# Four value products of 32 rows side by side, with softmax sums from added key halves, in a vision transformer block

## The chip, the cores and the metric

The kernel runs on one core of a Trainium2 chip. The metric is the time of one execution on the device in microseconds (us). An execution has five engines that run their own instruction streams and meet at semaphores: PE (TensorE: matmuls, and PEld, its weight loads), DVE (VectorE), ACT (ScalarE), POOL (GpSimd) and SP, which here issues DMAs.

## What is computed

128 images of 224x224x3 are cut into 14x14 patches, embedded into 192 numbers each, and given a class token: 197 tokens (padded to 198 in the kernel). One transformer block follows:

```python
h = tokens(x) ; h = concatenate([cls_tok, h])            # 128 x 197 x 192
n = layernorm(h)
q, k, v = (n @ W.T in 6 heads of 32)
scores = q k^T * 32**-0.5 + lam * (q . anchor_h)         # the same for all keys of a query
attn = softmax(scores) ; h = h + (attn @ v) @ Wo.T
x8 = clip(round(layernorm(h) / 0.02), -128, 127)         # int8
h = h + (x8 @ weight_t) * (0.02 * 0.01) + bias
```

## The kernel before

**Stages.** The first stage (`build_tokens`, up to about 429 us) embeds the patches and writes `h` and the normalised `xn` to scratch in HBM. The second (`build_attention`) takes the images one after the other and is the subject here.

**Steps.** Each engine runs the same loop over `i`: unrolled steps at both ends and a hardware loop over groups of six steps between. In one step an engine works on several images at once, each at another stage: f = i+5 (load and transpose of `xn`), a pair p of images (projection of q and k), a = i+1 (scores and their maxima), b = i (transposed scores, exponentials), c = i-1 (value products, transposes back, normalisation), e = i-2 (output projection, second layer norm), g = i-3 (quantising), k = i-4 (feed-forward product, output). A pair of images is projected in three blocks of 128 columns, two of them in an odd step (L894, L905) and one in an even step (L913). The order of work on each engine is the order in which its `step` writes it out; between engines there are semaphore waits only.

**Order on PE in a step (L883 to L996).** Scores 0 and 1 of a (`score`, L834, matmul L841); in an odd step block 0 into bank MISC[2]; the last transposed score of c, `score_t(c, 5)` (L896, matmul L853); block 1 or, in an even step, block 2 into MISC[2] (`project_block`, matmul L809); score 2; feed-forward (L924); value products of c (`attend`, L858, matmul L869); `score_t(b, 0)`; score 3; output projection of e (L829 to L831); `score_t(b, 1)`; transposes back (`turn_back`, L874, L879); transposes of `xn_in` into MISC[2] (L790); score 4; `score_t(b, 2)`; transposes of `qx`; transposes of `att`; score 5; `score_t(b, 3)`; value projection (L818); `score_t(b, 4)`; transposes of the maxima `max_parts` (L994).

**Scores twice.** `score` gives queries by keys, of which DVE takes the maximum per query (L1084). DVE splits the maxima into two parts (`max_parts`, a copy L1156 and a subtract L1158 of 99x12 elements), PE turns them, ACT copies them to `max_rows`, and SP sends them as rows into `q_st`. `score_t` gives keys by queries, with the maximum taken off by those two extra rows of the contraction, against ones in `k_st`. ACT takes the exponential of it (L1011) into `probs`, 99 keys by 2 halves of keys by 198 queries. Matmuls on fp32r operands are one record in the trace; those on fp32 operands are two.

**Value products.** `attend` multiplies `probs` by `vals`, tiles of 64 columns a head: 32 values, a column of ones (whose product is the softmax sum), and zeros. Two heads go to the upper and the lower 64 partitions of a bank of `o_bank`, three pairs of heads, two halves of the keys: 12 fp32 matmuls. ACT copies the result to `o_t` (L1037, L1038), six transposes bring it back to queries by heads, DVE takes the reciprocal (L1142) and multiplies (L1146) to `att`.

**DVE in a step (L1095 to L1180).** Maxima 0 and 1; the low parts `qk_lo` of the projected blocks (L1092) with maximum 2; `y` (L1117); two instructions on `qx` of g (L1122, L1125); maximum 3; `h1` of e (L1135); reciprocal and `att` of c; maxima 4 and 5; `max_parts`; statistics `st2` of e (L1164); `x_lo` of f (L1171), which reads bank MISC[2]; `a_lo` (L1179).

**POOL in a step (L1197 to L1223).** For e alone: `hb` = `h1` + bias (L1204), then after `st2` nine small instructions of the layer norm, each waiting for the one before (`norm_factors`, L139 to L147), then two of 99x192 that write `qx` (L1222), which DVE takes up in the next step.

**ACT in a step (L1020 to L1074).** High parts of the blocks (`high`, L1018), `exps(c, 5)`, `o_t`, `exps` 0, 1, 2 of b, `x_hi`, `exps(b, 3)`, `a_hi`, `exps(b, 4)`, `max_rows`, `qx_t`, `vals`.

**Ahead of the first step.** POOL finishes the last tokens' layer norm and fills two rows of `k_st` with ones (L1237); PE waits for these and for four constants of DVE (L998, L999).

Of the kernel before, what the change touches and what calls it, by code (L numbers as in the profile page):

```python
# [5 lines left out]
F32 = mybir.dt.float32  # L6
# [37 lines left out]
EARLY = 8  # L44

# [556 lines left out]
def build_attention(nc, s):  # L602
# [13 lines left out]
    HP = H // 2  # L616
    SPLIT = H - 4
    TW = 64
    OR = TW + HD + 1

# [10 lines left out]
    q_st = tile("q_st", [ST + 2, NP, H, 2, TP], F32R)  # L631
    k_st = tile("k_st", [ST + 2, NP, H, 2, TP], F32R)


    vals = tile("vals", [TC, NS, 2, H, TW])
# [4 lines left out]
    o_t = tile("o_t", [OR, NS, HP, TP])  # L640
# [29 lines left out]
    ones_made = sem("ones_made")  # L670
    last_row_ln = sem("last_row_ln")
# [15 lines left out]
    ln2_step, hb_done, passed = sem("ln2_step"), sem("hb_done"), sem("passed2")  # L687
    LN2_PER = 11
# [18 lines left out]
    with nc.Block() as block:  # L707
        @block.sync
        def _(sp):
# [11 lines left out]
            def step(i):  # L721
# [41 lines left out]
                if a.within(B):  # L763

                    sp.wait_ge(mrow_done, a.count(1, 1))
# [19 lines left out]
        def _(pe):  # L785
# [60 lines left out]
            def score_t(n, h):  # L846

                if h == 0:
                    pe.wait_ge(max_landed[n.slot], n.landed(16))
# [8 lines left out]
            def attend(n):  # L858

                pe.wait_ge(exp_done, n.count(H, H))  # L860
                pe.wait_ge(v_done, n.count(1, 1))
                if n.reuses(1):
                    pe.wait_ge(norm_done, n.count(1, 0))
                for p in range(HP):
                    for kc in range(2):
                        kk = TC if kc == 0 else NTOK - TC
                        for half in range(2):
                            h = 2 * p + half
                            last = pe.matmul(o_bank[half * TW:(half + 1) * TW, p // 2, (p % 2) * TP:(p % 2 + 1) * TP],  # L869
                                             vals[0:kk, n.two, kc, h, :], probs[0:kk, n.two, h, kc, :],  # L870
                                             start=kc == 0, stop=kc == 1)
                last.then_inc(av_done, 1)

            def turn_back(n):  # L874

                pe.wait_ge(ot_done, n.count(2, 2))
                for c in range(2):
                    for p in range(HP):
                        last = pe.transpose(o_bank[0:TC, c, 2 * TW * p:2 * TW * p + OR],  # L879
                                            o_t[:, n.two, p, c * TC:(c + 1) * TC], ident[0:OR, 0:OR])  # L880
                last.then_inc(back_done, 1)

            def step(i):  # L883
# [11 lines left out]
                if has_c:  # L895
# [10 lines left out]
                elif has_p:  # L906
# [6 lines left out]
                    project_block(MISC[2], p, 2)  # L913
                if has_a:
# [363 lines left out]
```

## Time and profile before

| | us |
|---|---|
| median of 3 runs | 1858.71 |
| lowest, highest | 1855.8, 1861.74 |
| the profiled execution's own time | 1860.42 |
| its span, first to last instruction | 1858.7 |

Busy shares of the span: PE 93%, PEld 86%, DVE 76%, ACT 42%, POOL 40%. The page divides the span into 40 slices; from the tenth on, PE's busy digit is 9 in all but two slices (its granted clock is at 9 or 8 tenths there on the page), with DVE at 7 and ACT at 5. In the tables of the trace a row has the start in us, its length in us, the engine, the line of the kernel, the operation, output and inputs by name, and shape; in square brackets stands the engine's idle time before it and what ended that. Matmuls overlap in the pipeline, so a matmul's length is longer than its distance to the next; distances of starts are what counts for PE. A granted clock of 1.00 is 2.4 GHz.

### The profile page before, as it was taken

The page shows a single profiled execution, that of the slowest core. Times are in us where ns is not written, and L with a number is a line of the kernel's source. Part 1 is how long each engine was busy: PE and PEld are TensorE (multiplying, and loading weights), DVE is VectorE, ACT ScalarE, POOL GpSimd, SP SyncE. Part 2 cuts the span into 40 slices and gives each one's busy share as a digit, 9 for nine tenths or more (in the row PEclk, how much of TensorE's full clock was granted, in tenths as well). Part 3 has the DMA queues.
Part 4 walks back from the last instruction along what each step waited for, and adds up shares of the span by engine and source line. Part 5 has one row for each costly group of instructions (what it writes and reads, how often), then busy time and mean ns, then how long its engine had stood idle before and what let it go on. Part 6 is the DMA issues. An engine that isn't in the chain of part 4 may idle for free.

```text
span 1858.7 us, 51623 instructions
## 1 busy us (share of the span) xinstructions
PE 1737.3 (93%) x15344; PEld 1602.8 (86%) x15344; DVE 1409.2 (76%) x3646; ACT 781.9 (42%) x1878; POOL 738.7 (40%) x1909
## 2 busy tenths in 40 slices
PE   1999999993899999999999999999999999999996
PEld 1999999993788888888888888888888888888885
DVE  4888888883577777777777777777777777777773
ACT  2000000000455555555555555555555555555552
POOL 3343543453033434334343344343443433434344
PEclk8999999996899999999999999999999999999997
DMA  9789998966677777777767777777787777777751
GB/s 282 207 284 305 304 314 285 312 212 150 115 135 137 140 132 132 135 138 135 135 127 137 136 135 138 127 137 136 134 138 131 134 135 137 135 135 127 134 99 31
DMA packets 214780, 303.57 MB, mean 163 GB/s; under 512 B 47585, under 2 KB 203636, under 8 KB 204613
## 3 DMA queue, kind: packets, MB, share of 16 engines
q1 hardware_dynamic: 204686, 228.05, 63.4%
q10 hardware_dynamic: 6054, 38.54, 7.3%
q0 software_dynamic: 3984, 36.28, 5.1%
q8 instruction: 30, 0.49, 0.1%
q14 instruction: 26, 0.20, 0.0%
HBM read 126.49 MB, written 58.29 MB: 99 GB/s over the span
## 4 chain that ended last, share of the span: by engine, by line
PE 62%; DVE 7%; issue 3%; POOL 2%; ACT 1%; SPq 1%; DMA 1%; DVEq 0%; POOLq 0%
PE o_bank L869 14%; PE bank L809 10%; PE bank L853 8%; PE bank L841 6%; PE bank L790 5%; PE o_bank L879 3%; PE bank L818 3%; PE o_bank L790 3%; PE bank L829 2%; PE bank L830 2%; PE bank L831 2%; PE bank L924 2%; DVE neg_max L1084 2%; DVE x_lo L1171 2%; ACT probs L1011 1%
## 5 line engine op out<-in xcount | busy, mean ns | idle before, releaser
L1011 ACT ACTIVATE probs<-bank 99x396 f32<-99x396 f32 x768 | 383.5, 499 | 245.3 <-PE bank L853 245.0
L1084 DVE TENSOR_REDUCE neg_max<-bank 99x2 f32<-99x394 f32 x768 | 420.2, 560 | 87.4 <-PE bank L841 86.0
L321 PE MATMUL bank<-e_t,xt 128*128 128x192 f32 x2352 | 386.8, 328 | 40.7 <-DVE xt L407 21.6
L321 PEld LDWEIGHTS bank<-e_t,xt 128*128 128x128 f32 x2352 | 385.2, 191 | 41.9 <-DVE xt L407 22.7
L853 PE MATMUL bank<-q_st,k_st 98*99 98x198 f32 x1536 | 284.3, 266 | 9.4 <-DMA q_st<-max_rows 4.1
L869 PE MATMUL o_bank<-probs,vals 99*64 99x198 f32 (+1 forms) x3072 | 289.0, 336 | 0.5 <-issue 0.3
L841 PE MATMUL bank<-k_st,q_st 96*99 96x198 f32 x1536 | 271.0, 272 | 14.6 <-DMA k_st<-qk_lo 9.7
L1204 POOL TENSOR_TENSOR hb<-h,ffn_bias 99x384 f32<-99x384 f32 x128 | 128.5, 1004 | 356.6 <-DVE h L1135 356.6
L869 PEld LDWEIGHTS o_bank<-probs,vals 99*64 99x64 f32 (+1 forms) x3072 | 211.8, 137 | 48.5 <-issue 1.2
L853 PEld LDWEIGHTS bank<-q_st,k_st 98*99 98x99 f32 x1536 | 202.4, 166 | 56.9 <-issue 36.6
L407 DVE STREAM_TRANSPOSE xt<-x_t 128x256 f32<-128x256 f32 x588 | 214.9, 416 | 43.3 <-PE bank L321 42.8
L1005 ACT ACTIVATE x_hi<-bank 128x396 fp32r<-128x396 f32 x128 | 63.3, 495 | 397.2 <-PE bank L790 397.2
L841 PEld LDWEIGHTS bank<-k_st,q_st 96*99 96x99 f32 x1536 | 195.6, 167 | 24.4 <-DMA k_st<-qk_lo 10.0
L1005 ACT ACTIVATE o_t<-o_bank 97x396 f32<-97x396 f32 (+1 forms) x256 | 93.1, 416 | 285.2 <-PE o_bank L869 285.2
L1092 DVE TENSOR_TENSOR qk_lo<-bank,qk_hi 128x396 fp32r<-128x396 f32 x192 | 108.8, 567 | 71.6 <-ACT qk_hi L1018 71.6
L1222 POOL TENSOR_SCALAR qx<-h,ln 99x192 f32<-99x192 f32 x256 | 127.0, 504 | 41.0 <-POOL ln L147 41.0
L1122 DVE TENSOR_SCALAR qx<-qx 99x384 f32<-99x384 f32 x128 | 46.1, 360 | 124.3 <-POOL qx L1222 124.3
L146 POOL TENSOR_TENSOR ln<-ln,minus_half 99x2 f32<-99x2 f32 (+2 forms) x143 | 127.4, 891 | 25.4 <-POOL ln L145 25.3
L139 POOL TENSOR_TENSOR ln<-st 99x2 f32<-99x2 f32 x128 | 25.2, 197 | 277.4 <-DVE st L1164 277.4
L1018 ACT ACTIVATE qk_hi<-bank 128x396 fp32r<-128x396 f32 x192 | 96.3, 502 | 90.6 <-PE bank L809 88.0
L829 PE MATMUL bank<-wo_hi,a_hi 96*99 96x192 f32 x512 | 130.0, 254 | 0.0
L830 PE MATMUL bank<-wo_lo,a_hi 96*99 96x192 f32 x512 | 129.9, 254 | 0.0
(121 smaller groups left out, 3426.4 us busy)
## 6 DMA issues: line engine op xcount, KB each, us to landing
x_t<-in_x_dram ACTq DMA_DIRECT2D x26, 1344.0 KB, 19.3
x_t<-in_x_dram SPq DMA_DIRECT2D x26, 1344.0 KB, 21.9
q_st<-qk_hi SPq DMA_DIRECT2D x128, 198.0 KB, 4.0
k_st<-qk_hi SPq DMA_DIRECT2D x128, 198.0 KB, 4.5
xn_in<-xn_scratch SPq DMA_DIRECT2D x128, 148.5 KB
h_in<-h_scratch SPq DMA_DIRECT2D x128, 148.5 KB
h_scratch<-h_t POOLq DMA_DIRECT2D x13, 1344.0 KB, 18.4
xn_scratch<-xn_t POOLq DMA_DIRECT2D x13, 1344.0 KB, 9.1
```

The costliest lines, as they stand in the source:

```text
L321: last = pe.matmul(token_bank(p)[:, 0:D], xt[:, p, c // 3, c % 3, :], e_t[:, row_kind(t), col, c // 3, c % 3, :], start=c == 0, stop=c == 5)
L407: last = nc.vector.transpose(xt[:, p, :, c, :].rearrange("p m (g b) -> p g m b", b=32), pix[:, c])
L790: last = pe.transpose(bank[0:width, ic * TP + c * TC:ic * TP + (c + 1) * TC], src[:, at, c, ic * width:(ic + 1) * width], ident[0:TC, 0:TC])
L809: last = pe.matmul(wide(bank, BLOCK), weights[:, Q:K + 1, :].rearrange("p w n -> p (w n)")[:, cols], inputs, start=i == 0, stop=i == len(p ...
L829: pe.matmul(acc, hi, wo_hi[:, ic, :], start=ic == 0, stop=False)
L830: pe.matmul(acc, hi, wo_lo[:, ic, :], start=False, stop=False)
L841: last = pe.matmul(S_BANK[h % 2][0:TC, c * TP:(c + 1) * TP], q_st[0:ST, n.pair, h, n.two, c * TC:(c + 1) * TC], k_st[0:ST, n.pair, h, n.tw ...
L853: last = pe.matmul(T_BANK[0:TC, c * TP:(c + 1) * TP], k_st[:, n.pair, h, n.two, c * TC:(c + 1) * TC], q_st[:, n.pair, h, n.two, :], start= ...
L869: last = pe.matmul(o_bank[half * TW:(half + 1) * TW, p // 2, (p % 2) * TP:(p % 2 + 1) * TP], vals[0:kk, n.two, kc, h, :], probs[0:kk, n.tw ...
L1005: nc.scalar.activation(dst, src, ACT.Copy, **affine).then_inc(done, 1)
L1011: nc.scalar.activation(probs[:, n.two, h, :, :], wide(T_BANK, TC), ACT.Exp).then_inc(exp_done, 1)
L1084: nc.vector.tensor_reduce(out=neg_max[:, n.two, :, h], in_=wide(S_BANK[h % 2], TC)[:, :, 0:NTOK], axis=AX_X, op=ALU.max, negate=True).then ...
```

## The change

- `vals` shrinks to 32 columns a head, without ones and zeros. `attend` writes 32 partitions a product: heads 0, 1, 4, 2 side by side over the first 198 columns of one bank; heads 3 and 5 over the next 198 columns, beside two tiles of softmax sums.
- The sums: a new tile `key_sum` holds the sum of the two halves of keys of `probs`. POOL adds heads 0 and 1, and 2 and 3, of image b; DVE adds heads 4 and 5 of image c. Six products of `key_sum` with `pick` (a column of ones at place j of 32 columns, else zeros) put the sums of the heads into rows. In all 18 fp32 matmuls. The first eight wait for five exponentials only, the others for the sixth and for the sums.
- As the padded key would now be counted, it gets a third extra row of the contraction: a score of -1e30 (`q_st` set by POOL to it ahead of the first step; `k_st` rows made on POOL as `key_rows`, copied by ACT into place). PE waits for ACT's copy only at its first transposed score.
- `o_t` is one tile of 128 partitions copied by one ACT instruction; four transposes of 128 columns go to the second bank. The wait for `mrow_done` moves from the products to the transposes back, the wait for `norm_done` of the image before is dropped.
- In even steps `score_t(c, 5)` and its exponential come after block 2.
- The rows of `Wo` are permuted on the host to the new order of heads (`HEAD_AT`).

```diff
+HEAD_AT = (0, 1, 4, 2, 3, 5)
...
-    vals = tile("vals", [TC, NS, 2, H, TW])
+    vals = tile("vals", [TC, NS, 2, H, HD])
+    pick = tile("pick", [TC, HG, HD])
...
-    o_t = tile("o_t", [OR, NS, HP, TP])
+    key_rows = tile("key_rows", [ST + 3, TP])
+    key_sum = tile("key_sum", [TC, NS, H, TP])
+    o_t = tile("o_t", [TILE, NS, 2, TP])
...
             def attend(n):
-                pe.wait_ge(exp_done, n.count(H, H))
+                def add_values(at, col, kc):
+                    h = HEAD_AT[at]
+                    kk = TC if kc == 0 else NTOK - TC
+                    pe.matmul(o_bank[at % 4 * HD:(at % 4 + 1) * HD, 0, col:col + TP], vals[0:kk, n.two, kc, h, :],
+                              probs[0:kk, n.two, h, kc, :], start=kc == 0, stop=kc == 1)
+
+                pe.wait_ge(exp_done, n.count(H, H - 1))
                 pe.wait_ge(v_done, n.count(1, 1))
-                if n.reuses(1):
-                    pe.wait_ge(norm_done, n.count(1, 0))
-                for p in range(HP):
-                    for kc in range(2):
-                        kk = TC if kc == 0 else NTOK - TC
-                        for half in range(2):
-                            h = 2 * p + half
-                            last = pe.matmul(o_bank[half * TW:(half + 1) * TW, p // 2, (p % 2) * TP:(p % 2 + 1) * TP],
-                                             vals[0:kk, n.two, kc, h, :], probs[0:kk, n.two, h, kc, :],
-                                             start=kc == 0, stop=kc == 1)
+                for kc in range(2):
+                    for at in range(4):
+                        add_values(at, 0, kc)
+                for j in range(HG):
+                    if j == 0:
+                        pe.wait_ge(exp_done, n.count(H, H))
+                        pe.wait_ge(pool_sums, n.count(2, 2))
+                    if j < 2:
+                        for at in (4, 5):
+                            add_values(at, TP, j)
+                    else:
+                        pe.wait_ge(dve_sums, n.count(1, 1))
+                    for side in range(2):
+                        to = (2 + side) * HD
+                        last = pe.matmul(o_bank[to:to + HD, 0, TP:2 * TP], pick[:, j, :],
+                                         key_sum[:, n.two, HEAD_AT[side * HG + j], :], start=j == 0, stop=j == HG - 1)
                 last.then_inc(av_done, 1)
 
             def turn_back(n):
-                pe.wait_ge(ot_done, n.count(2, 2))
+                pe.wait_ge(ot_done, n.count(1, 1))
                 for c in range(2):
-                    for p in range(HP):
-                        last = pe.transpose(o_bank[0:TC, c, 2 * TW * p:2 * TW * p + OR],
-                                            o_t[:, n.two, p, c * TC:(c + 1) * TC], ident[0:OR, 0:OR])
+                    for t in range(2):
+                        last = pe.transpose(o_bank[0:TC, 1, (2 * c + t) * TILE:(2 * c + t + 1) * TILE],
+                                            o_t[:, n.two, t, c * TC:(c + 1) * TC], ident[:, :])
                 last.then_inc(back_done, 1)
...
-                if has_c:
+                if has_c and (odd or not has_p):
                     score_t(c, 5)
...
                     project_block(MISC[2], p, 2)
+                    if has_c:
+                        score_t(c, 5)
...
+            def add_keys(n):
+                dve.wait_ge(exp_done, n.count(H, H))
+                if n.reuses(NS):
+                    dve.wait_ge(av_done, n.count(1, 1 - NS))
+                nc.vector.tensor_tensor(key_sum[:, n.two, 4:H, :], probs[:, n.two, 4:H, 0, :], probs[:, n.two, 4:H, 1, :],
+                                        ALU.add).then_inc(dve_sums, 1)
...
                     maxima(a, 1)
+                if has_c and not (has_p and not odd):
+                    add_keys(c)
                 if has_p and odd:
                     low(p, 0, MISC[2])
                 elif has_p:
                     low(p, 2, MISC[2])
+                    if has_c:
+                        add_keys(c)
...
+                def add_keys(first):
+                    pool.wait_ge(exp_done, b.count(H, first + 2))
+                    if first == 0 and b.reuses(NS):
+                        pool.wait_ge(av_done, b.count(1, 1 - NS))
+                    heads = slice(first, first + 2)
+                    nc.gpsimd.tensor_tensor(key_sum[:, b.two, heads, :], probs[:, b.two, heads, 0, :],
+                                            probs[:, b.two, heads, 1, :], ALU.add).then_inc(pool_sums, 1)
+
+                if b.within(B):
+                    add_keys(0)
...
                                         ffn_bias[:].unsqueeze(1).broadcast_to([TC, 2, D]), ALU.add).then_inc(hb_done, 1)
+                if b.within(B):
+                    add_keys(2)
                 pool.wait_ge(st2_done, e.count(1, 1))
...
-            pool.memset(k_st[ST:ST + 2, :, :, :, :].bitcast(F32), 1.0).then_inc(ones_made, 1)
+            pool.memset(q_st[ST:ST + 3, :, :, :, :].bitcast(F32), NO_SCORE).then_inc(no_score_made, 1)
```

## Rows read from the trace of the kernel before

**Rows 1.** Windows: busy PE, PEld, DVE, ACT, POOL (instructions), PEclk, DMA share, GB/s.

```profile
700.00:1700.00 1000.00, 977.31 (x9565) 884.39 (x9561) 772.84 (x1931) 563.38 (x1363) 401.96 (x1131) 1.00 0.76 135
```

**Rows 2.** Timeline of PE over an odd and an even step.

```profile
1206.77 0.42 PE L809 MATMUL bank<-x_hi,wa_hi 128*128 128x396 f32 x1 [0.39 <-DVE x_lo L1171]
...
1215.28 0.41 PE L841 MATMUL bank<-k_st,q_st 96*99 96x198 f32 x2
...
1217.57 0.43 PE L853 MATMUL bank<-q_st,k_st 98*99 98x198 f32 x2
1217.91 0.42 PE L809 MATMUL bank<-x_hi,wa_hi 128*128 128x396 f32 x1
...
1224.98 0.54 PE L790 MATMUL o_bank<-ident,att 99*96 99x99 f32 x4
1225.30 0.40 PE L841 MATMUL bank<-k_st,q_st 96*99 96x198 f32 x2
...
1227.92 0.42 PE L809 MATMUL bank<-x_hi,wa_hi 128*128 128x396 f32 x1 [0.34 <-DVE x_lo L1171]
```

**Rows 3.** Timeline of DVE over the same steps.

```profile
1211.26 0.36 DVE L1122 TENSOR_SCALAR qx<-qx 99x384 f32<-99x384 f32 x1 [0.51 <-POOL qx L1222]
...
1216.63 0.61 DVE L1164 BATCH_NORM_STATS2 st<-h 99x6 f32<-99x192 f32 x2
1217.16 0.61 DVE L1171 TENSOR_TENSOR x_lo<-bank,x_hi 128x198 fp32r<-128x198 f32 x2
...
1222.41 0.36 DVE L1122 TENSOR_SCALAR qx<-qx 99x384 f32<-99x384 f32 x1 [1.27 <-POOL qx L1222]
...
1226.55 0.17 DVE L1158 TENSOR_TENSOR max_parts<-neg_max,max_parts 99x12 fp32r<-99x12 f32 x1
```

**Rows 4.** Timeline of POOL over the even step.

```profile
1217.32 0.20 POOL L139 TENSOR_TENSOR ln<-st 99x2 f32<-99x2 f32 x1 [2.31 <-DVE st L1164]
...
1221.38 0.99 POOL L1222 TENSOR_SCALAR qx<-h,ln 99x192 f32<-99x192 f32 x2 [0.31 <-POOL ln L147]
1224.19 1.01 POOL L1204 TENSOR_TENSOR hb<-h,ffn_bias 99x384 f32<-99x384 f32 x1 [1.81 <-DVE h L1135]
```

**Rows 5.** Timeline of PE, two narrow windows at the first value products.

```profile
1209.47 0.39 PE L869 MATMUL o_bank<-probs,vals 99*64 99x198 f32 x2
...
1209.47 0.56 PE L869 MATMUL o_bank<-probs,vals 99*64 99x198 f32 x4
```

**Rows 6.** The chain that ended last: start, length, what.

```profile
1207.92 0.19 PE bank L853 x2
...
1209.54 2.17 PE o_bank L869 x24
...
1213.51 0.52 PE o_bank L879 x6
```

**Rows 7.** Timeline of ACT over the two steps.

```profile
1208.35 0.49 ACT L1011 ACTIVATE probs<-bank 99x396 f32<-99x396 f32 x1
...
1223.57 0.50 ACT L1011 ACTIVATE probs<-bank 99x396 f32<-99x396 f32 x1 [0.67 <-PE bank L853]
...
1225.93 0.50 ACT L1011 ACTIVATE probs<-bank 99x396 f32<-99x396 f32 x1 [0.23 <-PE bank L853]
```

**Rows 8.** First stage: two timelines at 83 us, two lines' durations (min/median/max ns).

```profile
83.24 0.68 POOL L586 TENSOR_SCALAR xn_t<-h_t,ln 128x192 f32<-128x192 f32 x1
...
83.58 0.55 DVE L390 SCALAR_TENSOR_TENSOR wb<-w_raw,wb 64x192 fp32r<-64x192 f32 x1
...
L586 POOL TENSOR_SCALAR xn_t<-h_t,ln x3: 512/600/682, 82.8 to 83.9; 128x192 f32<-128x192 f32 x3
...
L393 DVE TENSOR_TENSOR wb<-w_raw,wb x2: 355/356/356, 77.5 to 89.9; 64x192 fp32r<-64x192 f32 x2
```

**Rows 9.** Timelines of PE and of SP at the second stage's start.

```profile
441.31 0.89 PE L790 MATMUL bank<-ident,xn_in 99*128 99x99 f32 x4 [13.91 <-POOL k_st L1237]
...
438.27 0.39 SPq L719 DMA_DIRECT2D xn_in<-xn_scratch  x1
```

More of the change, by code:

```diff
@@ L630, in build_attention @@
     qk_lo = tile("qk_lo", [BLOCK, 3, 2 * TP], F32R)
-    q_st = tile("q_st", [ST + 2, NP, H, 2, TP], F32R)
-    k_st = tile("k_st", [ST + 2, NP, H, 2, TP], F32R)
-    vals = tile("vals", [TC, NS, 2, H, TW])
+    q_st = tile("q_st", [ST + 3, NP, H, 2, TP], F32R)
+    k_st = tile("k_st", [ST + 3, NP, H, 2, TP], F32R)
+    vals = tile("vals", [TC, NS, 2, H, HD])
+    pick = tile("pick", [TC, HG, HD])
     neg_max = tile("neg_max", [TC, NS, 2, H])
@@ L763, in step @@
                 if a.within(B):
+                    if a.fixed and a.n == 0:
+                        sp.wait_ge(no_score_made, 1)
                     sp.wait_ge(mrow_done, a.count(1, 1))
@@ L1026, in step @@
                     high(p, 0, MISC[2])
-                if has_c:
+                if has_c and (odd or not has_p):
                     exps(c, 5)
@@ L1032, in step @@
                     high(p, 2, MISC[2])
+                    if has_c:
+                        exps(c, 5)
                 if has_c:
@@ L1036, in step @@
                         act.wait_ge(back_done, c.count(1, 1 - NS))
-                    copy(o_t[:, c.two, 0:2, :], o_bank[0:OR, 0, 0:2 * TP].rearrange("p (a n) -> p a n", a=2), ot_done)
-                    copy(o_t[:, c.two, 2, :], o_bank[0:OR, 1, 0:TP], ot_done)
+                    copy(o_t[:, c.two, :, :], wide(o_bank[:, 0, :], TILE), ot_done)
                 if has_b:
@@ L1072, in step @@
                         act.wait_ge(av_done, a.count(1, 1 - NS))
-                    copy(vals[:, a.two, :, :, 0:HD],
+                    copy(vals[:, a.two, :, :, :],
                          MISC[1][0:TC, 0:2 * D].rearrange("p (c h d) -> p c h d", c=2, h=H), v_done)
+            act.wait_ge(rows_made, 2)
+            copy(k_st[ST:ST + 3, :, :, :, :].rearrange("p a h s n -> p (a h s) n"),
+                 key_rows[ST:ST + 3, :].unsqueeze(1).broadcast_to([3, 2 * NP * H, TP]), ones_made)
             images(act, step)
@@ L1180, in step @@
                                             a_hi[:, c.two, :, :].bitcast(F32), ALU.subtract).then_inc(alo_done, 1)
-            nc.vector.memset(vals[:], 0.0).then_inc(consts, 1)
+            nc.vector.memset(pick[:], 0.0).then_inc(consts, 1)
             dve.wait_ge(consts, 1)
-            nc.vector.memset(vals[:, :, :, :, HD:HD + 1], 1.0).then_inc(consts, 1)
+            for j in range(HG):
+                nc.vector.memset(pick[:, j, j:j + 1], 1.0).then_inc(consts, 1)
             dve.wait_ge(last_row_ln, 9)
@@ L1223, in step @@
                                             v[6][:, cc:cc + 1], ALU.add, ALU.mult).then_inc(ln2_step, 1)
+            pool.memset(key_rows[ST:ST + 3, :], 1.0).then_inc(rows_made, 1)
+            pool.wait_ge(rows_made, 1)
+            pool.affine_select(out=key_rows[ST:ST + 3, 0:NTOK], in_=key_rows[ST:ST + 3, 0:NTOK], compare_op=ALU.is_ge,
+                               fill=0.0, base=1, pattern=[[0, NTOK]], channel_multiplier=-1).then_inc(rows_made, 1)
+            pool.wait_ge(rows_made, 2)
             made = [0]
```

30 lines of the change are left out of this document (19 added, 11 removed).

## The prediction

> **What bounds the kernel now.** I read the sums over the steady stretch first: TensorE (PE) busy 977 of 1000 us at a granted clock of 1.00, which is 2.4 GHz, the next engine at 77% [rows 1]. So PE is the first suspect; but at 98% it is full only if nothing waits, and what an edit to PE's work is worth depends on what ends each wait. So next the order of time on PE over two steps [rows 2]. Steps come in two kinds: odd ones project two blocks (L809), even ones one. I cut a pair at two marks: L809's first matmul, and the fifth score (L841, `score(a, 5)`). Odd work: 1206.77 to 1215.28 = 8.51 us; then 2.63 to the next L809 (1217.91); even work 7.39 (to 1225.30); then 2.62 (to 1227.92). A pair is 21.15 us.
>
> The two gaps of 2.62 are no PE sum. L809 starts 0.14 us after `x_lo` ends (1217.16 + 0.61 = 1217.77, [rows 3]), in both kinds of step; PE idles 0.39 and 0.34 there. `x_lo` is at the end of VectorE's queue after max, `max_parts`, `st2`. So the gap is **DVE's latency from the fifth score**.
>
> The even work of 7.39 has a second limit, a loop through three engines. From the fifth score (1215.28) `st2` is done at 1217.24; GpSimd (POOL) starts its chain 0.08 later, at 1217.32 [rows 3, 4]; chain and `qx` end at 1221.38 + 0.99 = 1222.37; DVE, idle for 1.27 us until then, starts `qx` at 1222.41; then max, h1, reciprocal and `att` lead to PE's turn of `att` at 1224.98 and the fifth score at 1225.30 [rows 2, 3]. That is 2.04 + 5.05 + 0.04 + 2.89 = 10.02 us, which is just the step (7.39 + 2.63). In even steps PE and this **loop** end together, so PE time saved there is worth nothing; in odd steps the loop has 1.1 us to spare.
>
> **The change, part by part.** *Value products.* Now 12 fp32 matmuls, recorded as 24, two side by side; a pair starts each 0.17 us (0.39, 0.56 us for 2, 4) [rows 5], 12 pair starts, 2.17 us in all [rows 6]. After it, 18 matmuls, 36 records, four side by side: two rounds of four heads, two rounds of two heads with two sums, one round of two sums. Five rounds of two records are 10 starts: 2 x 0.17 = 0.34 us less. Nothing here shows four at once; from below it is 0.34, from above 18 starts if only two run together (+1.02 us). I take the 0.34, since the two of now start together with no loss.
>
> *Transposes back.* Six took 0.52 us [rows 6]; four remain, with 128 columns for 97: between 0 and 0.17 less, I take 0.08. The single o_t copy spares ScalarE an instruction where PE has a score and the output projection before it needs the result: nothing.
>
> *The moved score.* In even steps `score_t(c, 5)` stands at 1217.57, in the time in which L809 waits for `x_lo` anyway [rows 2]. Behind L809 its 0.19 us [rows 6] is added to the even work. The wait for the exponential that it passes was not the last one ahead of L809. Cost: +0.19 even, bounds 0 and 0.19.
>
> *Key sums.* Two adds on POOL of 99x396, one on DVE. POOL takes 1.00 us for the add of 99x384 at 1224.19 [rows 4], so 1.03 each. The first waits for the second exponential of image b, which ends at 1223.57 + 0.50 = 1224.07 [rows 7]; it and `hb` behind it end by 1226.2. The second waits for the fourth, 1225.93 + 0.50 = 1226.43, so with POOL's 0.08 it starts at 1226.51 and ends at 1227.54, while the chain behind it on POOL would have started at 1227.33. That is 0.2 us on the loop. The wait has in its queue the layer norm chain, for which DVE's `qx`, and behind that all of DVE, waits. DVE's add waits for `exps(c, 5)` (1208.35 + 0.49 in odd steps, [rows 7]), with low, max and y behind it; DVE has 0.51 (odd) and 1.27 us (even) before `qx` [rows 3] and the add takes about 0.55: just covered. PE's new waits for these sums have the first score of the next image behind them; POOL's are over before the step begins, DVE's add about 0.5 us before PE's last round in even steps and 1.5 in odd ones. The wait for the maxima's row copy, moved from the products to the transposes back, is met before either place.
>
> *The collision.* POOL's second add starts at 1226.51; DVE's `max_parts` subtract (L1158), with both inputs in SBUF, starts at 1226.55 [rows 3]. What happens then is shown once in the prologue [rows 8]: a DVE instruction with two SBUF inputs, started at 83.58 among POOL's normalising of rows, took 0.55 instead of 0.36 us, and POOL's took 0.68 and 0.60 instead of 0.51. They take turns. There the DVE instruction got what was left of POOL's short one; it came free when POOL's reads were over. L1158 would stand behind nearly all of a 1.03 us add: end at 1227.55 instead of 1226.72, **0.83 us late**. Everything in DVE's queue moves with it: `st2` (so the chain), `x_lo` (so L809), `mpart_done` (so PE's transposes of maxima, which then have 0.7 us to wait).
>
> The Trainium skill, page "SBUF — State Buffer", section "Who interferes with whom", says that a DVE instruction with two SBUF inputs and a GpSimd instruction that reads SBUF exclude each other for the whole instruction, by order of issue. By it the delay is the same 0.83; with sharing by halves, which the prologue rows do not exclude for so long an add, it would be about 0.2.
>
> Who is first? POOL leads by 0.04 us, and from the two stalls in the prologue (POOL's of 0.17 in the row of 83.24, behind the DVE instruction in front of 83.58, and DVE's of 0.19 at 83.58) both engines need about equally long from a start to the first read. So I take POOL as first, in both kinds of step.
>
> *Sum.* Odd: 8.51 - 0.34 - 0.08 = 8.09 of PE work, gap 2.62 + 0.83 = 3.45: 11.54 us. Even: PE would need 7.39 + 0.19 - 0.42 + 3.45 = 10.61, the loop 10.02 + 0.83 = 10.85 (the add is over before the late chain starts): 10.85. A pair is 22.39, +1.24; 0.62 us an image. 126 of the 128 images are in this state: +78 us.
>
> *Start of the stage.* PE's wait of 13.9 us for POOL's memset of `k_st` ends at 441.31 [rows 9]. The memset leaves PE's path, but the input loads, the first image's last issued at 438.27 + 0.39, land only some 1.5 to 2 us later, and two small POOL instructions (about 0.8 us) now stand ahead of the chain that leads to them: bounds -1 and +1 us, taken as 0. The new copy on ScalarE (some 7 us) lies beside that. The memset of `q_st` is over long before the first maxima.
>
> The profiled execution was 1860.4 us, 1.7 above the median of 1858.7: 1860.4 + 78 - 1.7 = **1937 us**. If the add takes 0.99 to 1.24 us, it is 1932 to 1963.
>
> **Rivals.** (1) POOL and DVE don't disturb each other here. Then odd is 8.09 + 2.62 = 10.71; even the loop with the 0.2 of POOL, 10.22; pair 20.93, -0.22: -14 us, 1845. For it: the overlap in the prologue is only one place, and L393 ran in 0.36 us beside POOL's power. This is the **other side**, faster, and what decides is whether L1158 waits. (2) They exclude each other, but DVE is first. L1158 is on time; then DVE's new add (at about 2.1 us after L809) keeps POOL's chain waiting some 0.4 us: even loop 10.02 + 0.25 + 0.4 = 10.67, odd 10.71, pair +0.23: +14, 1873. (3) POOL first in one kind of step alone: the odd gap without the 0.83, pair +0.41: +26, 1885. (4) The POOL loop isn't a limit: odd 10.71, even 7.16 + 2.62 = 9.78: pair -0.66, -42: 1817. Against it: the 1.27 us for which DVE waits for `qx`, and `att` that PE takes 0.06 us after it could be ready. (5) Four narrow products don't run together, only two, with 18 starts. Then odd is 8.51 + 1.02 - 0.08 + 2.62 = 12.07, even 7.39 + 0.19 + 0.94 + 2.62 = 11.14, pair +2.06: +130, 1988. The gain of the products is gone from a start distance of 0.20 us on (10 x 0.20 = 12 x 0.17).
>
> On (5), the Trainium skill, page "TensorE: Matmul & The Clock Gate", section "Measured speedup vs the span model", has four row tiles at 3.07 times and three column tiles at 2.38 times one, not 4 and 3. By the first, a start of four would be 0.17 x 4 / 3.07 = 0.22 us (an estimate), over the 0.20 just named; its own model of 4 ns per further tile puts that down to fill and drain, and then nothing is lost. This trace has two only.
>
> **How the numbers follow.** Forecast 0.50 (shown interference, lead of 0.04 us). (1) 0.18. (2) 0.11. (3) 0.08. (4) 0.07. (5) 0.06. The range leaves out (4) and (5): 1843 to 1957, the top from a longer add. A measurement of this kernel tells 0.3%, 5.6 us, from no change. Faster by more: most of (1) and all of (4), 0.21. Within: rest of (1) and a part of (2), 0.07. Slower: 0.72.
>
> **What would show it.** Right: L1158 at about 1.0 us instead of 0.17, PE waiting for DVE ahead of L994, L809's idle time over 0.4 us in both kinds, steps of about 11.5 and 10.9 us; L869 with 36 records in about 1.8 us. Wrong: L1158 at 0.17 and POOL's second add longer than 1.03 (rival 2), both at their length (rival 1), L869 over 2.2 us (rival 5), DVE not waiting for `qx` in even steps (rival 4).

## The result, and the profile after

| | before | after |
|---|---|---|
| median of 4 runs, us | 1859.34 | 1912.79 |
| lowest, highest | 1855.8, 1861.74 | 1910.57, 1913.83 |
| the profiled execution's own time | 1860.42 | 1910.57 |
| its span | 1858.7 | 1909.0 |

The ratio is 1.0282 (95% interval 1.027 to 1.0294): 53.5 us slower, where 78 were forecast. The changed kernel has fewer starts of value products and is still slower, so the place to look is where PE waits. The windows row for 700 to 1700 us (busy PE, PEld, DVE, ACT, POOL with instructions; granted clock; DMA share; GB/s) answers [rows 1]:

```profile
700.00:1700.00 1000.00, 919.80 (x10122) 801.36 (x10120) 836.72 (x1952) 534.24 (x1226) 544.30 (x1274) 1.00 0.75 129
```

PE went from 977 to 920 us of 1000 at the same granted clock of 1.00, DVE from 773 to 837, POOL from 402 to 544. The timeline of PE over an even and an odd step answers [rows 2] (L817 is `project_block`, before L809; L849 `score`, before L841; L1018 the transposes of the maxima, before L994):

```profile
1200.32 0.42 PE L817 MATMUL bank<-x_hi,wa_hi 128*128 128x396 f32 x1
...
1207.28 0.55 PE L798 MATMUL o_bank<-ident,att 99*96 99x99 f32 x4
1207.60 0.41 PE L849 MATMUL bank<-k_st,q_st 96*99 96x198 f32 x2
...
1209.78 0.34 PE L1018 MATMUL o_bank<-ident,max_parts 99*12 99x99 f32 x2 [0.48 <-DVE max_parts L1197]
1210.93 0.42 PE L817 MATMUL bank<-x_hi,wa_hi 128*128 128x396 f32 x1 [0.45 <-DVE x_lo L1210]
...
1222.38 0.43 PE L817 MATMUL bank<-x_hi,wa_hi 128*128 128x396 f32 x1 [0.44 <-DVE x_lo L1210]
```

The two marks of the prediction cut it: even work 1200.32 to 1207.60 = 7.28, gap 3.33 (to 1210.93); odd work 8.12 (its fifth score, `score(a, 5)`, starts at 1219.05 in the same view), gap 3.33 again. PE's work fell, both gaps grew from 2.62 to 3.33, and a new wait stands in them, for `max_parts`. DVE's timeline shows what is late there (L1197 is the subtract, before L1158; it answers [rows 3]):

```profile
1208.65 0.17 DVE L1195 CAST max_parts<-neg_max 99x12 fp32r<-99x12 f32 x1
1208.86 0.86 DVE L1197 TENSOR_TENSOR max_parts<-neg_max,max_parts 99x12 fp32r<-99x12 f32 x1
1209.65 0.61 DVE L1203 BATCH_NORM_STATS2 st<-h 99x6 f32<-99x192 f32 x2
1210.18 0.61 DVE L1210 TENSOR_TENSOR x_lo<-bank,x_hi 128x198 fp32r<-128x198 f32 x2
```

A subtract of 12 columns takes 0.86 us instead of 0.17, and `st2` and `x_lo` follow it. Both its inputs lie in SBUF, the memory of the kernel's tiles; the banks that PE writes its results to are PSUM. Beside it on POOL ([rows 4]; L1245 is the key add, L140 the start of the layer norm chain, before L139):

```profile
1206.53 0.89 POOL L1245 TENSOR_TENSOR key_sum<-probs 99x396 f32<-99x396 f32 x1 [1.77 <-DVE h L1173]
1207.37 1.01 POOL L1257 TENSOR_TENSOR hb<-h,ffn_bias 99x384 f32<-99x384 f32 x1
1208.81 0.88 POOL L1245 TENSOR_TENSOR key_sum<-probs 99x396 f32<-99x396 f32 x1 [0.43 <-ACT probs L1034]
1210.34 0.20 POOL L140 TENSOR_TENSOR ln<-st 99x2 f32<-99x2 f32 x1 [0.64 <-DVE st L1203]
```

POOL's add starts at 1208.81, 0.05 us ahead of the subtract, and ends at 1209.69; the subtract ends at 1209.72. The subtract's own view (durations in ns: least, median, most; first and last start) and the waits from 700 to 1700 us (total us, times, longest; 91 images lie in it) say that it is not this step alone:

```profile
L1197 DVE TENSOR_TENSOR max_parts<-neg_max,max_parts x128: 172/868/876, 472.3 to 1869.8; 99x12 fp32r<-99x12 f32 x128
PE o_bank L1018 <- DVE max_parts L1197: 44.7, 91, 0.5
PE bank L817 <- DVE x_lo L1210: 32.1, 76, 0.5
DVE qx L1160 <- POOL qx L1277: 34.0, 45, 0.8
```

Of 128 subtracts 126 take 0.86 us or more; only those of the first two images take 0.17. Before, the median was 171 ns. From first start to last there are 127 intervals: (1869.8 - 472.3) / 127 = 11.00 us an image; before, the same line ran from 472.5 to 1819.6, 10.61. The difference, 1397.5 - 1347.1 = 50.4 us, is the whole difference of the two spans (50.3).

The products are what they were meant to be. The chain that ended last (start, length, what), against [rows 6]:

```profile
1202.19 0.97 PE o_bank L873 x18
...
1203.66 0.35 PE o_bank L892 x6
...
1205.63 0.19 PE bank L863 x2
1205.81 0.44 PE o_bank L901 x4
```

`attend` runs from 1202.19 to 1204.01, 1.82 us for 36 records where 24 took 2.17; the transposes back take 0.44 where they took 0.52. Three windows ending later and later in the first products answer [rows 5]:

```profile
1202.12 0.38 PE L873 MATMUL o_bank<-probs,vals 99*32 99x198 f32 x4
...
1202.12 0.54 PE L873 MATMUL o_bank<-probs,vals 99*32 99x198 f32 x8
...
1202.12 0.71 PE L873 MATMUL o_bank<-probs,vals 99*32 99x198 f32 x12
```

Four tiles of 32 columns start together (within 0.02 us), and the next four 0.16 to 0.17 us later, as the growth of the window's length shows: the distance that two tiles of 64 had before.

### The profile page after: what moved, and what is told of

Its sections match the earlier page's. It is cut to its first block, busy times and chain, and to the rows that moved or that the text cites. A ratio compares the mean times of both kernels' runs of the same rounds, so it can differ in the third digit from the quotient of the medians.

```text
span 1909.0 us, 54954 instructions
## 1 busy us (share of the span) xinstructions
PE 1704.6 (89%) x16624; PEld 1528.9 (80%) x16624; DVE 1537.4 (81%) x3776; ACT 773.6 (41%) x1751; POOL 961.5 (50%) x2167
## 4 chain that ended last, share of the span: by engine, by line
PE 55%; DVE 13%; issue 6%; DMA 1%; POOL 1%; SPq 0%; DVEq 0%; ACT 0%; POOLq 0%; ACTq 0%
PE bank L817 11%; PE o_bank L873 10%; PE bank L863 6%; PE bank L849 6%; PE bank L798 5%; DVE neg_max L1111 4%; DVE st L1203 3%; PE o_bank L798 3%; PE o_bank L901 3%; DVE x_lo L1210 3%; PE o_bank L892 3%; PE bank L839 2%; PE bank L837 2%; PE bank L838 2%; PE bank L948 2%
## 5 line engine op out<-in xcount | busy, mean ns | idle before, releaser
L1245 POOL TENSOR_TENSOR key_sum<-probs 99x396 f32<-99x396 f32 x256 | 227.2, 888 | 377.3 <-ACT probs L1034 373.8
L863 PE MATMUL bank<-q_st,k_st 99*99 99x198 f32 x1536 | 281.1, 264 | 6.0 <-DMA q_st<-max_rows 3.7
L849 PE MATMUL bank<-k_st,q_st 96*99 96x198 f32 x1536 | 271.2, 272 | 16.2 <-DMA k_st<-qk_lo 10.7
L863 PEld LDWEIGHTS bank<-q_st,k_st 99*99 99x99 f32 x1536 | 207.7, 167 | 50.2 <-issue 43.9
L849 PEld LDWEIGHTS bank<-k_st,q_st 96*99 96x99 f32 x1536 | 193.4, 167 | 24.5 <-DMA k_st<-qk_lo 11.0
L873 PE MATMUL o_bank<-probs,vals 99*32 99x198 f32 (+1 forms) x3072 | 199.6, 338 | 0.0
L1028 ACT ACTIVATE k_st<-key_rows 3x7128 fp32r<-3x7128 f32 x1 | 6.1, 6139 | 382.5 <-POOL key_rows L1285 382.5
L1028 ACT ACTIVATE o_t<-o_bank 128x396 f32<-128x396 f32 x128 | 64.0, 500 | 228.0 <-PE o_bank L892 228.0
L892 PE MATMUL o_bank<-key_sum,pick 99*32 99x198 f32 x1536 | 152.7, 333 | 0.0
L873 PEld LDWEIGHTS o_bank<-probs,vals 99*32 99x32 f32 (+1 forms) x3072 | 113.9, 110 | 47.5 <-issue 0.2
L147 POOL TENSOR_TENSOR ln<-ln,minus_half 99x2 f32<-99x2 f32 (+2 forms) x143 | 128.1, 896 | 25.4 <-POOL ln L146 25.3
L839 PE MATMUL bank<-wo_hi,a_lo 96*99 96x192 f32 x512 | 129.9, 254 | 0.0
```

What stands on the lines that cost most here:

```text
L839: last = pe.matmul(acc, lo, wo_hi[:, ic, :], start=False, stop=ic == 1)
L849: last = pe.matmul(S_BANK[h % 2][0:TC, c * TP:(c + 1) * TP], q_st[0:ST, n.pair, h, n.two, c * TC:(c + 1) * TC], k_st[0:ST, n.pair, h, n.tw ...
L863: last = pe.matmul(T_BANK[0:TC, c * TP:(c + 1) * TP], k_st[:, n.pair, h, n.two, c * TC:(c + 1) * TC], q_st[:, n.pair, h, n.two, :], start= ...
L873: pe.matmul(o_bank[at % 4 * HD:(at % 4 + 1) * HD, 0, col:col + TP], vals[0:kk, n.two, kc, h, :], probs[0:kk, n.two, h, kc, :], start=kc == ...
L892: last = pe.matmul(o_bank[to:to + HD, 0, TP:2 * TP], pick[:, j, :], key_sum[:, n.two, HEAD_AT[side * HG + j], :], start=j == 0, stop=j == ...
L1245: nc.gpsimd.tensor_tensor(key_sum[:, b.two, heads, :], probs[:, b.two, heads, 0, :], probs[:, b.two, heads, 1, :], ALU.add).then_inc(pool_ ...
```

## The experiments

The theory: POOL's second key add keeps DVE's subtract waiting because that has both inputs in SBUF; the subtract's 0.7 us goes straight into the gap of both kinds of step. The rivals: POOL's adds cost by their place in POOL's queue (they hold up its chain); or the loss is in the products or in the moved score. Where "the changed kernel" is edited, the rest of it stays.

### Take the adds out, and put them alone into the kernel before

`e1_no_pool_adds`, on the changed kernel, leaves POOL's two adds out, and PE's wait for them:

```diff
+            pool.memset(key_sum[:, :, 0:4, :], 1.0).then_inc(pool_sums, 1)
...
-                if b.within(B):
-                    add_keys(0)
...
-                if b.within(B):
-                    add_keys(2)
```

> The changed kernel without POOL's two adds (the sums of heads 0 to 3 are left out: key_sum holds ones there, so those heads come out wrong). Theory (DVE's max_parts subtract, both inputs in SBUF, waits while POOL's second add reads SBUF, and all of DVE's queue with it): the subtract takes 0.17 us instead of 0.86, the gap from the fifth score to L817 falls from 3.33 to 2.62 us, odd steps 8.12 + 2.62 = 10.74, even steps by the loop over POOL's chain 9.97; pair 20.7 instead of 22.06, 63 pairs: about 1828 us. Rival (the narrow products or the moved score cost the time): about 1910 us, gap still 3.3.

Measured: 1829.98 us, ratio to before 0.9836 (0.982 to 0.9853). The subtract is back at 0.17 us (128 times 170 to 175 ns), gaps are 2.63, even work 7.29, odd work 8.10 in the steps cut.

`e3_before_plus_adds`, on the kernel before: POOL's two adds as in the change, their result unused; ACT writes a `probs` tile again only when POOL has read it.

```diff
+                def add_keys(first):
+                    pool.wait_ge(exp_done, b.count(H, first + 2))
+                    heads = slice(first, first + 2)
+                    nc.gpsimd.tensor_tensor(key_sum[:, b.two, heads, :], probs[:, b.two, heads, 0, :],
+                                            probs[:, b.two, heads, 1, :], ALU.add).then_inc(pool_sums, 1)
...
+                    act.wait_ge(pool_sums, n.count(2, 2 - 2 * NS))
```

> The kernel before with nothing but POOL's two adds of key halves put in; their result is not used. Theory: DVE's subtract L1158 takes about 0.86 us instead of 0.17, the gap 3.33 instead of 2.62, odd 8.51 + 3.33 = 11.84, even 10.72; pair 22.56 instead of 21.15: about 1948 us. Rival (adds on POOL are harmless by themselves, since it is 60% idle): the chain starts at most 0.07 us later, about 1862 us.

Measured: 1948.13 us, ratio 1.0477 (1.0459 to 1.0494). DVE's and POOL's timelines of it:

```profile
1207.27 0.87 DVE L1161 TENSOR_TENSOR max_parts<-neg_max,max_parts 99x12 fp32r<-99x12 f32 x1
...
1207.22 0.89 POOL L1206 TENSOR_TENSOR key_sum<-probs 99x396 f32<-99x396 f32 x1 [0.51 <-ACT probs L1014]
```

So the parts nearly add: everything but POOL's adds is worth -30 us (1829.98 against 1859.74, the kernel before timed beside it), the adds +83 on the changed kernel and +88 on the kernel before. The products and the moved score are not where the loss is. The kernel without adds isn't quite the floor: four kernels below have a POOL instruction in that place, which holds nothing up, and take 1825 us; their even steps average 9.93 to 9.96 us from 700 to 1700 us, this one's 9.99. Why is open.

### Leave the add, and change who is first

`e2_add_behind_max_parts`: POOL's second add waits for DVE's subtract.

```diff
+                    if first == 2 and i.plus(1).within(B):
+                        pool.wait_ge(mpart_done, i.plus(1).count(2, 2))
```

> The changed kernel with POOL's second add also waiting for max_parts, so that DVE's subtract goes first. All work is done. Theory: the subtract takes 0.17 us, the gap is 2.62; the add ends 2.35 us after the fifth score, the chain begins at 2.4 instead of 2.04, even steps 10.3, odd 10.74; pair 21.05: about 1849 us. If DVE's add of keys keeps POOL's chain waiting, 0.4 more in even steps, about 1875. Rival (what costs is POOL's longer queue ahead of the chain, not who is first): no faster than 1913, since the add now comes later.

Measured: 1864.23 us, ratio 1.0022 (1.0012 to 1.0031), between the two numbers. The gap is 2.63 in both kinds; the pair is 21.18 us (odd 8.07 + 2.63, even 7.85 + 2.63). The even steps lose by the loop, in two places of POOL's queue:

```profile
1201.25 0.95 POOL L147 TENSOR_TENSOR ln<-ln,minus_half 99x2 f32<-99x2 f32 x1 [0.18 <-POOL ln L146]
...
1208.22 0.89 POOL L1247 TENSOR_TENSOR key_sum<-probs 99x396 f32<-99x396 f32 x1 [1.33 <-DVE max_parts L1197]
1209.07 0.19 POOL L140 TENSOR_TENSOR ln<-st 99x2 f32<-99x2 f32 x1
...
1201.08 0.56 DVE L1118 TENSOR_TENSOR key_sum<-probs 99x396 f32<-99x396 f32 x1
```

The chain starts 2.35 us after the fifth score (1206.72; 2.03 without adds), and its power (L147) takes 0.95 us where it takes 0.70: DVE's own key add (last row above), two inputs in SBUF, had started 0.17 us before it. Over 700 to 1700 us the power's mean is 946 ns here, 704 in the changed kernel, where DVE's key add starts 0.14 us *after* the power:

```profile
1212.99 0.70 POOL L147 TENSOR_TENSOR ln<-ln,minus_half 99x2 f32<-99x2 f32 x1 [0.18 <-POOL ln L146]
...
1213.13 0.57 DVE L1118 TENSOR_TENSOR key_sum<-probs 99x396 f32<-99x396 f32 x1 [0.92 <-ACT probs L1034]
```

Neither is longer here: 0.70 and 0.57. So the same exclusion is seen with the roles exchanged, but not for as long as the power is busy. That the power is done with its few reads within 0.14 us would explain it; this is argued from the rows, and no run varied it.

### Reads or writes

`e4_memset_for_add`: the second add is a write of 99x850.

```diff
+                    if first == 2:
+                        pool.sem_inc(passed, 1)
+                        nc.gpsimd.memset(junk[:], 1.0).then_inc(pool_sums, 1)
+                        return
```

> The changed kernel with POOL's second add replaced by a memset of 99x850 (0.8 us by the rate of the memset of k_st before, 0.85 ns an element), which only writes SBUF; the sums of heads 2 and 3 are left out (wrong there). Theory in its narrow form (the two share a way to read): the subtract takes 0.17 us, the gap is 2.62, about 1830 us. Wide form (any POOL instruction on SBUF holds DVE's two-input ones up): subtract about 0.8 us, gap about 3.25, about 1908 us.

Measured: 1825.05 us, ratio 0.9817 (0.98 to 0.9833), the subtract at 0.17. But it started at 1206.53 and the memset at 1206.56: DVE was first by 0.03 us, so the order alone could explain it. (The memset starts 0.16 us after the exponential that it waits for, the add of the changed kernel 0.08.) The run didn't tell the two apart. `e6_memset_early` was to: the memset is longer and doesn't wait for the exponential.

```diff
-                    pool.wait_ge(exp_done, b.count(H, first + 2))
+                    if first == 0 or not e.within(B):
+                        pool.wait_ge(exp_done, b.count(H, first + 2))
...
+    junk = tile("junk", [TC, 1300])
```

> Leaves work out: POOL's second add is a memset of 99x1300 that writes SBUF and reads nothing, so the sums of heads 2 and 3 are those of a constant. Unlike the run with the memset of 99x850, it does not wait for the fourth exponential: it follows the bias add at once, starts about 0.5 us ahead of DVE's max_parts subtract and takes about 1.24 us, so it is running when the subtract starts. If only a POOL instruction that reads SBUF keeps the subtract waiting, the subtract takes 0.17 us again and the time is about 1825 us (1822 to 1832). If what counts is merely which of the two started first (in the earlier memset run DVE was 0.03 us ahead), the subtract ends with the memset, about 0.55 us late, in both kinds of step: 126 x 0.55 = +69 us, about 1895 us (1880 to 1905).

Measured: 1912.55 us, ratio 1.0271 (1.0255 to 1.0286). Neither number. The timelines of DVE and POOL name another instruction:

```profile
1209.77 0.87 DVE L1197 CAST max_parts<-neg_max 99x12 fp32r<-99x12 f32 x1
1210.68 0.17 DVE L1199 TENSOR_TENSOR max_parts<-neg_max,max_parts 99x12 fp32r<-99x12 f32 x1
...
1209.42 1.19 POOL L1250 MEMSET junk<- 99x1300 f32 x1
```

The copy ahead of the subtract, SBUF to SBUF, ended with the memset (1210.64 and 1210.61), and the subtract came after both. In 120 of 128 images the copy takes over 0.5 us. In the changed kernel the copy ends as POOL's add starts (1208.82 and 1208.81) and keeps its 0.17; whether an add would hold it up was not tried. Two more kernels separate copy and subtract. Both use the version below that keeps the maxima in PSUM, so that the copy reads PSUM; in `e7_psum_memset_early` the subtract has one SBUF input, in `e8_memset_early_two_sbuf` two:

```diff
-                    nc.vector.tensor_tensor(lo, neg_max[:, :, a.two, :, :], hi.bitcast(F32),
+                    nc.vector.tensor_tensor(lo, hi.bitcast(F32), hi.bitcast(F32),
```

> The kernel with the maxima in PSUM, and POOL's second add replaced by the early memset of 99x1300 (the sums of heads 2 and 3 are those of a constant). In the earlier run with this memset it was DVE's CAST of the maxima, an SBUF to SBUF copy, that waited (0.87 to 0.98 us where it takes 0.17), and the subtract behind it, started after the memset had ended, did not. Here the copy reads PSUM and the subtract has one SBUF input. If it is the copy's two SBUF sides that a POOL write excludes, both take 0.17 us beside the running memset and the time is that of the kernel with the maxima in PSUM, 1825 us (1820 to 1830). If any DVE instruction writing SBUF or any start under a POOL memset waits, the copy takes about 0.8 us again: about 1825 + 126 x 0.6 = 1900 us (1885 to 1915).

> As the kernel with the maxima in PSUM and the early memset, but the subtract takes the copy's result for both its inputs, hi - hi, so both are in SBUF (the low part of the maxima is zero, and the sums of heads 2 and 3 are those of a constant). The memset of 99x1300 starts some 0.4 us before the copy and runs through copy and subtract, so the subtract with two SBUF inputs starts under a POOL instruction that only writes. If only POOL's reads exclude it: copy and subtract 0.17 us each, 1825 us (1820 to 1830). If any POOL instruction already running excludes it: the subtract waits for the memset's end, about 0.5 us, +126 x 0.5 = 63: 1888 us (1875 to 1900).

Measured: 1825.25 us (ratio 0.981, 0.9794 to 0.9826) and 1825.55 us (0.9815, 0.9799 to 0.9831). DVE and POOL of the second:

```profile
1208.16 0.17 DVE L1200 CAST max_parts<-s_bank 99x12 fp32r<-99x12 f32 x1
1208.37 0.18 DVE L1202 TENSOR_TENSOR max_parts<-max_parts 99x12 fp32r<-99x12 f32 x1
...
1207.69 1.19 POOL L1252 MEMSET junk<- 99x1300 f32 x1
```

Both start inside a memset that runs from 1207.69 to 1208.88, and neither waits. So a POOL instruction that only writes holds up the SBUF to SBUF copy, and not the subtract with two SBUF inputs, nor a copy out of PSUM. As `e9_psum_two_sbuf` below shows, this same form of the subtract does wait beside POOL's add; what excludes it is therefore that POOL reads. (The run with the memset of 99x850 would thus have had 0.17 in either order.)

### Take the cause away with all the work done

`v1_max_in_psum`: the row maxima stay in spare columns of the two PSUM banks that the scores use.

```diff
-        banks = [ctx.enter_context(nc.psum_tensor(f"bank{i}", [128, 512], F32)) for i in range(6)]
+        s_bank = ctx.enter_context(nc.psum_tensor("s_bank", [128, 2, 512], F32))
+        banks = [s_bank[:, 0, :], s_bank[:, 1, :]]
...
-    neg_max = tile("neg_max", [TC, NS, 2, H])
+    neg_max = s["s_bank"][0:TC, :, 2 * TP:2 * TP + NS * H].rearrange("p b (t c k) -> p b t c k", t=NS, c=2)
```

> The changed kernel with all its work, except that the row maxima are kept in spare columns of the two PSUM banks that the scores use (the two banks become one tensor), so that the max_parts subtract has one input in PSUM and only one in SBUF. POOL's second key add stays where it is. If the subtract of the changed kernel waits because both its inputs come from SBUF while POOL reads SBUF, it takes about 0.2 us here beside the add of 0.88; the gap from the fifth score to the next projection falls from 3.33 to about 2.65, odd steps to 10.75, even steps to the loop of about 9.95 to 10.1: 126/2 pairs of 20.75 against 22.06, 1912.8 - 82 = 1831 us, between 1825 and 1838. Rival A: with the subtract on time, DVE's own key add falls beside POOL's power and stretches it, as in the run with the add behind the subtract; with the chain starting at the earlier time of the run without POOL's adds this was not seen, but if it is, even steps lose 0.2 to 0.4 us: 1843 to 1858. Rival B: any DVE instruction waits behind a POOL add, whatever it reads: the subtract stays at 0.86 and the time at 1913 (bounds 1905 to 1915, PSUM reads being slightly longer).

Measured: 1824.56 us (5 runs, 1823.94 to 1826.97), ratio to before 0.9798 (0.9785 to 0.9812). It came just below the expected 1825 to 1838. This version beats both kernels: 2.0% faster than before, and 0.9798 / 1.0282 = 0.953 of the change's time. Its windows row, and DVE and POOL at the place:

```profile
700.00:1700.00 1000.00, 965.17 (x10786) 856.00 (x10788) 825.74 (x2080) 558.04 (x1307) 575.64 (x1355) 1.00 0.78 138
...
1209.78 0.17 DVE L1200 TENSOR_TENSOR max_parts<-s_bank,max_parts 99x12 fp32r<-99x12 f32 x1
...
1209.72 0.89 POOL L1247 TENSOR_TENSOR key_sum<-probs 99x396 f32<-99x396 f32 x1 [0.48 <-ACT probs L1036]
1210.57 0.20 POOL L142 TENSOR_TENSOR ln<-st 99x2 f32<-99x2 f32 x1
```

The add is first by 0.06 us, as in the changed kernel, and the subtract takes 0.17. Even steps are 9.94 (7.31 + 2.63), odd ones 10.75 (8.11 + 2.64). To exclude that the new place of the maxima brings the gain in another way, `e9_psum_two_sbuf` gives this version's subtract two SBUF inputs, by the edit of `e8_memset_early_two_sbuf`, beside the real add:

> The kernel with the maxima in PSUM and POOL's real adds, but the subtract takes the copy's result for both its inputs, hi - hi (the low part of the maxima is zero). It differs from that kernel in where the first input of this one 99x12 instruction lies. In that kernel DVE's subtract started 0.05 us after POOL's add, as in the changed kernel. If two SBUF inputs are what makes it wait behind the add: the subtract takes about 0.86 us, the gap is 3.3 us again and the time 1905 to 1915 us, taken as 1911. If the gain of the maxima in PSUM came from something else (the place of the maxima, the start times), the subtract stays at 0.17 and the time at 1825 us. If the subtract and the add trade places in some steps, since they start within 0.05 us, it lies between.

Measured: 1912.94 us, ratio 1.0281 (1.0264 to 1.0298). Where one operand of one instruction of 12 columns lies is worth 88 us (the subtract takes 0.85 us or more in 126 of 128 images):

```profile
1211.21 0.87 DVE L1200 TENSOR_TENSOR max_parts<-max_parts 99x12 fp32r<-99x12 f32 x1
...
1211.16 0.89 POOL L1247 TENSOR_TENSOR key_sum<-probs 99x396 f32<-99x396 f32 x1 [0.44 <-ACT probs L1036]
```

### The moved score

`e5_score_back`, on the changed kernel, and `v2_max_in_psum_score_back`, on the version with the maxima in PSUM:

```diff
-                if has_c and (odd or not has_p):
+                if has_c:
                     score_t(c, 5)
...
-                    if has_c:
-                        score_t(c, 5)
```

> The changed kernel with only the sixth score of the next image and its exponential put back ahead of the projection in even steps. In the changed kernel the late subtract is in the loop as well as in the gap (even 10.61 = 7.28 + 3.33), and PE waits only 0.1 us for att in even steps, so the loop is what ends them: 0 to -0.1 us per even step, -6 to 0, so 1907 to 1913 us, taken as 1910. Rival: PE's sum ends the even steps: -0.16 x 63 = -10 us, 1903 us, with the wait for att grown. Second rival: the earlier exponential lets DVE's key add run earlier, beside POOL's power of the layer norm: the chain is stretched by 0.15 to 0.25 us, +9 to +16 us, 1922 to 1929.

> The kernel with the maxima in PSUM, and in even steps the sixth score of the next image and its exponential back ahead of the projection, as in the kernel before. In even steps the end is set by the loop through POOL's chain, not by PE's sum, so the 0.16 us that the moved score puts on PE's even work buys nothing: the same time as the one without this edit, within 3 us. Rival: PE's sum sets the even steps too; then 63 even steps x 0.16 us = 10 us less. A second rival: DVE's key add, which waits for this exponential, starts earlier by up to 1 us in even steps and no longer fits its idle time ahead of qx as it does now: a change of either sign up to 10 us.

Measured: 1913.23 us (ratio 1.0272, 1.0258 to 1.0286) against 1912.79, and 1825.93 against 1824.56. No gain in either. In `e5_score_back` PE reaches `att` earlier and waits for it (the starts of the two turns are 0.65 us apart here, 0.47 in the changed kernel):

```profile
1207.88 0.52 PE L798 MATMUL bank<-ident,qx 99*96 99x99 f32 x4
1208.53 0.55 PE L798 MATMUL o_bank<-ident,att 99*96 99x99 f32 x4
```

## Why the prediction was right, and where its size was off

**What bounds it.** Right. The gap after the fifth score is DVE's latency: a subtract 0.69 us longer made it 0.71 longer (2.62 to 3.33) in both kinds of step, though PE's own work had shrunk. The loop ends the even steps, where DVE waits for POOL's `qx`: by the prediction's four terms it is now 2.73 (fifth score to chain start) + 5.04 (1199.72 to 1204.76) + 0.03 + 2.81 (1204.79 to 1207.60) = 10.61, the step of 7.28 + 3.33:

```profile
1199.72 0.20 POOL L140 TENSOR_TENSOR ln<-st 99x2 f32<-99x2 f32 x1 [0.64 <-DVE st L1203]
...
1203.77 0.99 POOL L1277 TENSOR_SCALAR qx<-h,ln 99x192 f32<-99x192 f32 x2 [0.31 <-POOL ln L148]
...
1204.79 0.36 DVE L1160 TENSOR_SCALAR qx<-qx 99x384 f32<-99x384 f32 x1 [0.74 <-POOL qx L1277]
```

**Products, transposes, moved score.** -0.35, -0.08 and 0.19 us, against -0.34, -0.08 and 0.19. Odd work was put at 8.09 and is 8.12. The trace has a start of four each 0.16 to 0.17 us, so rival (5), 1988 us, is out. The Trainium skill, page "TensorE: Matmul & The Clock Gate", section "Measured speedup vs the span model", stood beside this: worked out from its 3.07 times for four row tiles, a start would be 0.22 us (an estimate), which these products do not bear out; its model of some 4 ns for each further tile fits them better (the four of a start are 6 to 7 ns apart here). That the difference between the two is fill and drain was the prediction's reading, and that section doesn't say it.

**The collision.** Right in mechanism, place, order and in both kinds of step: POOL led by 0.05 us (0.04 forecast) and the subtract ended with the add. What the prologue rows showed once [rows 8] holds 126 times. The lead was thin, though: the memset of 99x850, which waits for the same exponential, came 0.03 us behind the subtract. So which of the two is first hangs on a margin of 0.05 us, and that it fell as forecast is in part luck. The Trainium skill, page "SBUF — State Buffer", section "Who interferes with whom", says that a DVE instruction with two SBUF inputs and a GpSimd instruction that reads SBUF exclude each other whole, by order of issue. Here both orders are measured (0.17 to 0.86 one way, the power's 0.70 to 0.95 the other), and its "reads" too: the memset leaves the same subtract at 0.18. Its "whole instruction" holds for the adds and not for the power, beside which DVE's key add wasn't held up. The trace of the kernel before has the same in its prologue, a DVE subtract with two SBUF inputs at its usual length inside a long power of POOL:

```profile
76.94 2.78 POOL L146 TENSOR_TENSOR ln<-ln,minus_half 128x15 f32<-128x15 f32 x1 [0.18 <-POOL ln L145]
...
77.46 0.35 DVE L393 TENSOR_TENSOR wb<-w_raw,wb 64x192 fp32r<-64x192 f32 x1
```

The same section says that a DVE copy or cast can run in a mode that uses both pairs of ports, one of which it shares with GpSimd, and then contends with it. The copy held up by the early memset agrees with that (0.87 us instead of 0.17), though no run here shows in which mode it ran; the forecast had not thought of the copy.

**The size.** The forecast had +1.24 us a pair, 78 us. The two profiled executions differ by 50.3 us; the medians differ by 53.5, and the 3 us between lie within the spread of the runs (1855.8 to 1861.7 before). Four things took 78 to 50; the first is the term of the sum that was mis-sized.
- The add. The prediction scaled POOL's 1.00 us for `hb` [rows 4] to 1.03; the key add takes 0.88 (256 times, mean 888 ns). The delay is then 0.69 and not 0.83: 0.14 x 126 = 18 us. `hb` reads its bias through a broadcast; that this is why it is slower for fewer elements was not tested.
- From DVE's `qx` to the fifth score it is 2.81 us, not 2.89: 0.08 x 63 = 5 us.
- The odd work is 8.12 and not 8.09, which gives 2 us back.
- One pair was taken as the mean. The cut pairs are 21.15 and 22.06 us, +0.91; the means over the stage are 21.21 and 22.01, +0.79. That is 0.12 x 63 = 7 us.

18 + 5 - 2 + 7 = 28, and 78 - 28 = 50, the 50.3 of the spans. The start of the stage, taken as 0, is 0.5 us earlier: PE's first transposes are at 440.80 instead of 441.31 [rows 9], and what they wait for is now the image's DMA, as forecast.

**The rivals.** (1), no disturbance, 1845 us, did not happen, but the version with the maxima in PSUM is that case, and it came at 1825: the 0.2 us by which the second add was to hold up the chain isn't there, since an add of 0.88 ends when `st2` does (chain 2.05 us after the fifth score). (2), DVE first, 1873 us, was made with the added wait and came at 1864: the power lost 0.25 us, not 0.4. (3) is out, both kinds are hit. (4), the loop no limit, is out: DVE still waits 0.74 us for `qx` in even steps, and the score put back brought nothing. The range's top, 1957, stood below the 1963 that the same text has for its longest add; the add was shorter, and it didn't matter.

## What to carry to other kernels

Ahead of moving work to POOL, list the DVE instructions that it will lie beside and look where their inputs are. In these runs one with two SBUF inputs, though only 12 columns wide, waited for the end of a POOL add that had started 0.05 us earlier. If it stands in the latency that the next step waits for, the cost is nearly the POOL instruction's length in every step (0.69 of 0.88 us), although PE is the fullest engine. The other order, DVE first, was better but moved part of the wait to POOL (1864 us). What repaired it was to have one of the inputs in PSUM, where the scores' own two banks had room for 12 more columns each (1825 us).

## What the runs showed that was not expected

- A POOL memset, which reads nothing, held an SBUF to SBUF copy of 99x12 for 0.70 us (0.87 instead of 0.17), and let the same copy out of PSUM, and a subtract with two SBUF inputs, pass at 0.17 and 0.18.
- POOL adds two tiles of 99x396 in 0.888 us, but 99x384 and a broadcast bias in 1.006.
- A lead of 0.05 us is enough: POOL's add was first by that much, and the subtract waited in 126 of 128 images.
